# Another order of steps in each slot of a transformer encoder's software pipeline, on one core

## What is computed

```python
L, D, H, F = (4, 128, 16, 512)
for i in range(L):
    xn = layer_norm(x, ln1_w[i], ln1_b[i])
    x = x + mha(xn, mask, in_proj_w[i], in_proj_b[i], out_proj_w[i], out_proj_b[i])   # causal, ALiBi
    xn = layer_norm(x, ln2_w[i], ln2_b[i])
    h = jax.nn.gelu(xn @ ffn1_w[i].T + ffn1_b[i], approximate=False)
    x = x + (h @ ffn2_w[i].T + ffn2_b[i])
return layer_norm(x, final_w, final_b)
...
x = x + _L0_attn_ref(xn, ...) + _L0_ffn_ref(xn, ...)
```

## Time and profile before

| | us |
|---|---|
| median of three executions | 1640.66 |
| lowest, highest | 1640.59, 1646.0 |
| the profiled execution, its time | 1640.9 |
| its span in the trace | 1639.1 |
| busy in the span: PE, DVE, ACT, POOL | 1421.8, 1131.8, 1223.2, 614.3 |

### The profile page before, as it was taken

How to read it: one execution, slowest core, us unless ns; L and a number is a source line. 1 busy time by engine, 2 the same in 40 slices (tenths; PEclk the granted TensorE clock), 3 DMA queues, 4 the chain that set the end, 5 groups by cost and what they waited for, 6 DMA issues and landing times.

```text
span 1639.1 us, 38563 instructions
## 1 busy us (share of the span) xinstructions
PE 1421.8 (87%) x10720; PEld 946.2 (58%) x10720; DVE 1131.8 (69%) x2851; ACT 1223.2 (75%) x2165; POOL 614.3 (37%) x1052
## 2 busy tenths in 40 slices
PE   0677787568999999999999999999999989999995
PEld 0445554335666666666666666666666656666653
DVE  6567676347777777677677766777776767777762
ACT  3233333238999898898999888999888988888884
POOL 5232222123333343333333333334333345555443
PEclk9999888779999999999999999999999999999997
DMA  3332333045444444444444445444444444444430
GB/s 107 100 114 89 107 92 101 24 122 149 121 124 127 117 116 126 134 129 119 120 129 119 122 121 133 129 119 121 127 119 123 129 128 125 124 125 125 123 90 10
DMA packets 104789, 187.60 MB, mean 114 GB/s; under 512 B 19912, under 2 KB 70728, under 8 KB 104720
## 3 DMA queue, kind: packets, MB, share of 16 engines
q1 hardware_dynamic: 89904, 150.45, 33.3%
q0 software_dynamic: 14848, 36.72, 8.3%
HBM read 120.87 MB, written 65.01 MB: 113 GB/s over the span
## 4 chain that ended last, share of the span: by engine, by line
PE 53%; DVE 17%; issue 14%; DMA 9%; POOL 2%; DVEq 1%; ACT 1%; SPq 1%; POOLq 0%; ACTq 0%
PE pvp L979 11%; PE exp_ps L956 7%; DVE negm L698 6%; PE mxp L923 6%; PE dense L1009 6%; PE dense L1018 5%; PE dense L868 5%; DMA blocks<-split_L 4%; PE mxp L927 4%; DVE xn L666 3%; PE dense L896 2%; PE dense L997 2%; DVE ost L744 2%; PE mxp L868 2%; DMA blocks<-negt 2%
## 5 line engine op out<-in xcount | busy, mean ns | idle before, releaser
L831 ACT ACTIVATE probs<-exp_ps 128x512 f32<-128x512 f32 x896 | 525.0, 593 | 289.1 <-PE exp_ps L956 286.4
L698 DVE TENSOR_REDUCE negm<-mxp 128x2 f32<-128x512 f32 x896 | 569.2, 683 | 90.3 <-PE mxp L927 72.6
L956 PE MATMUL exp_ps<-qbd_l,kst_l 128*128 128x512 f32 x768 | 368.5, 495 | 8.3 <-issue 4.3
L923 PE MATMUL mxp<-blocks,qst 104*128 104x512 f32 x768 | 325.5, 453 | 34.5 <-DMA blocks<-split_L 19.7
L855 ACT ACTIVATE exp_ps<-masktf 128x512 f32<-128x512 f32 x513 | 308.8, 602 | 22.6 <-DVE rest L766 6.5
L927 PE MATMUL mxp<-maskb,identb 128*128 128x256 bf16 (+1 forms) x768 | 247.6, 322 | 0.0
L498 POOL TENSOR_SCALAR veps<-mv 128x2 f32<-128x2 f32 x144 | 31.7, 220 | 560.9 <-DVE mv L657 557.2
L923 PEld LDWEIGHTS mxp<-blocks,qst 104*128 104x128 f32 x768 | 149.0, 194 | 84.2 <-DVE negm L698 37.0
L979 PE MATMUL pvp<-probs,vst_l 128*32 128x256 f32 (+1 forms) x4096 | 194.5, 330 | 0.6 <-ACT probs L831 0.6
L744 DVE COPY ost<-pvp 128x512 f32<-128x512 f32 x80 | 55.3, 692 | 201.6 <-PE pvp L979 201.6
L956 PEld LDWEIGHTS exp_ps<-qbd_l,kst_l 128*128 128x128 f32 x768 | 144.4, 195 | 40.8 <-issue 31.3
(11 more groups left out here) (95 smaller groups left out, 2006.6 us busy)
## 6 DMA issues: line engine op xcount, KB each, us to landing
split_L<-hi SPq DMA_DIRECT2D x256, 128.0 KB, 2.1
qst<-split_L SPq DMA_DIRECT2D x64, 384.0 KB
kst_l<-split_L SPq DMA_DIRECT2D x64, 384.0 KB
qbd_l<-split_L SPq DMA_DIRECT2D x256, 96.0 KB
split_L<-lo POOLq DMA_DIRECT2D x128, 128.0 KB, 2.1
blocks<-split_L SPq DMA_DIRECT2D x128, 96.0 KB
blocks<-split_L POOLq DMA_DIRECT2D x128, 96.0 KB, 4.4
split_F<-hi SPq DMA_DIRECT2D x64, 128.0 KB, 2.1
```

Of the source, the lines that this page charges most:

```text
L698: dve.tensor_reduce(heads[:, g, first:first + count], mxp[:, (plan.max_chunks * g + ch) % 3, :].rearrange("p (h t) -> p h t", h=count), AX ...
L831: act.activation(probs[:, g[0], ch, :], exp_ps[:, (plan.exp_chunks * g[0] + ch) % 2, :], ACT.Exp, scale=plan.scale).then_inc(q.b_exp, 1)
L923: pe.matmul(mxp[:, bank, :], qst[0:BIAS_END, g[0], qt * P:(qt + 1) * P], kbd[0:BIAS_END, first:first + count, g[0], 0:keys], start=True, s ...
L956: pe.matmul(exp_ps[:, bank, :], kst[plan.name][:, s, g[0], kt * P:(kt + 1) * P], rhs, start=not on_diagonal, stop=True, skip_group_check=T ...
```

## The change

The steps are split into finer ones, and each has its own place in the list: `ln` and `rstd` (now at slot `s+3`), `xb`, `xb2`, `rstd2`, `y`, `hi`, `lo`, `hi>`, `row>`, `smax>`, `smaxp`, `f1` and `f2` in two halves, `gelu` in two. Since an engine takes from the list only the steps in which it has a part, each has an order of its own. A step such as `xt+` can stand in the list ahead of `xt`: ACT's part has its place among ACT's steps.

In the encoder's slot the maxima begin behind `op` and the first `pv`, and go one by one up to the slot's end. `negt` stands behind the last of them, three of the four `pv` and `v` behind it. `ln` is taken one slot earlier. `end` and `end+` stand ahead of `op+`.

Dense products use all five banks by a table `banks`; `take` makes PE wait for the bank's last reader, whoever that was. The maxima use banks 2 to 4. `SEEDER` names ACT for all eight seeds, as before. The weights come in five parts (`qk`, `v`, `o`, `w1`, `w2`), each loaded at `w:part` after its last use (`last_use`) and waited for at `w=part`; only the slots with `s == 0` wait for them. PE, ACT and DVE run the encoder in two loops, and one round earlier than before (-2).

```diff
-    def __init__(self, name, heads, causal, feed_forward, rounds):
+    def __init__(self, name, heads, causal, feed_forward, rounds, banks):
...
             return (
-                exps[0:2] + at("ot", s - 1) + at("ln", s + 2) + at("ot+", s - 1) + at("v v+", s + 1) + at("xn", s + 2)
-                + at("f2 f2+", s - 2) + at("at at+", s - 1)
-                + exps[2:3] + maxes[0:2] + at("xt", s + 2)
...
-                + exps[9:10] + at("xt2 xt2+", s - 1) + values[0:2] + end2
-                + exps[10:11] + at("negt negt+", s + 1) + at("stack_max+", s + 2)
-                + exps[11:12] + at("f1 f1+", s - 1) + values[2:4] + at("pv+", s) + store)
+                part("exp", s, 0) + at("xn", s + 2) + part("f2", s - 2, 0)
+                + part("exp", s, 1) + at("v+", s + 1) + at("w:v", s + 2) + at("ot+", s - 1) + at("ln", s + 3)
+                + at("f2+", s - 2) + end + at("xb ot", s - 1)
+                + part("exp", s, 2) + part("f2", s - 2, 1) + at("w:w2 xb2 rstd2 at at+", s - 1)
+                + end2 + at("op+ w=w1", s - 1)
+                + part("exp", s, 3, 4) + at("lo xt+", s + 2) + at("op", s - 1) + at("w:o", s) + at("stack>", s + 1)
+                + at("w=v hi>", s + 2) + part("pv", s, 0) + at("row>", s + 1) + part("max", s + 1, 0) + at("xt", s + 2)
+                + part("max", s + 1, 1)
+                + part("exp", s, 5) + at("w=w2", s - 1) + part("max", s + 1, 2) + at("rstd", s + 3)
+                + part("exp", s, 6) + at("y", s + 2) + at("xn2", s - 1) + at("qk", s + 2) + at("w:qk", s + 3)
+                + part("max", s + 1, 3) + at("hi", s + 2)
+                + part("exp", s, 7, 8) + at("w=o", s) + part("max", s + 1, 4) + at("xt2", s - 1) + at("smaxp", s + 2)
+                + part("max", s + 1, 5, 6) + at("xt2+", s - 1) + part("max", s + 1, 7)
+                + part("exp", s, 9) + part("max", s + 1, 8)
+                + part("exp", s, 10) + part("max", s + 1, 9) + part("f1", s - 1, 0) + part("max", s + 1, 10)
+                + part("exp", s, 11) + at("w=qk", s + 3) + part("max", s + 1, 11) + at("negt+", s + 1)
+                + part("gelu", s - 1, 0) + part("f1", s - 1, 1) + at("negt", s + 1) + part("pv", s, 1, 2, 3)
+                + at("smax>", s + 2) + at("pv+", s) + part("gelu", s - 1, 1) + at("w:w1", s) + at("v", s + 2) + store)
...
+    "xt": 0, "qk": 1, "v": 1, "at": 3, "op": 3, "xt2": 0, "negt": 2, "f2": 4, "ot": 0, "f1": (0, 1)})
...
+        bank = dense + [mxp[:, k, :] for k in range(3)]
...
+            def row_of_maxima(plan, q, u, s):
+                sp.wait_ge(q.b_negt, u + 1)
+                settle(sp, passed_sp)
+                wait_past(sp, q.b_s, plan.exp_chunks * GROUPS * (u - 1))
+                settle(sp, passed_sp)
+                sp.dma_start(qbd[plan.name][MAX_ROW:MAX_ROW + 1, s, :, :].bitcast(F32),
+                             negt[0:plan.heads, s, :, :].bitcast(F32)).then_inc(q.nmax[s], 16)
...
-                def dense_job(bank, sem, count, unit_offset, done=None):
-                    if read[bank] is not None:
-                        before, per_round, constant = read[bank]
+                def take(number, sem, count, unit_offset, done=None):
+                    if read[number] is not None:
+                        before, per_round, constant = read[number]
                         pe.wait_ge(before, per_round * n + constant)
-                    read[bank] = (sem, 2 * count, count * unit_offset + (count if done is None else done))
+                    read[number] = (sem, 2 * count, count * unit_offset + (count if done is None else done))
+                    return bank[number]
```

More of the change, by code:

```diff
@@ L65, in __init__ @@
         self.units = 2 * rounds
-        self.at_bank = 0 if causal else 1
     def max_bank(self, ch):
@@ L79, in at, with part @@
             return [(name, unit) for name in names.split()]
-        exps = [("exp", s, *divmod(k, self.exp_chunks)) for k in range(self.exp_chunks * GROUPS)]
-        maxes = [("max", s + 1, *divmod(k, self.max_chunks)) for k in range(self.max_chunks * GROUPS)]
-        values = [("pv", s, g) for g in range(GROUPS)]
+        def part(name, unit, *numbers):
+            return [(name, unit, k) for k in numbers]
         if self.causal:
@@ L396, in expert_round, with load_weights @@
                     share(EXPERT, S["F"], step, u, s, r)
+            q, per = S["L"], BATCH // 2
+            def load_weights(part, layer):
+                which, first, end = WEIGHTS[part]
+                to, source = (wa["L"], wa_l) if which == "a" else (wc["L"], wc_l)
+                sp.dma_start(to[:, first:end], source[layer][:, first:end]).then_inc(q.w[part], 16)
             rounds_of(sp, EXPERT, expert_round)
-            q, per = S["L"], BATCH // 2
-            sp.dma_start(wa["L"][:], wa_l[0]).then_inc(q.wa, 16)
+            for part in WEIGHTS:
+                load_weights(part, 0)
             sp.wait_ge(S["F"].c_done, BATCH)
@@ new lines, in _ @@
+            for k in (-2, -1, 0, 1):
+                encoder_round(0, k)
+            with sp.Fori(2, per - 2) as k:
+                encoder_round(0, k, inner=True)
+            encoder_round(0, per - 2)
+            encoder_round(0, per - 1)
+            with sp.Fori(1, LAYERS - 1) as layer:
+                encoder_round(layer, 0)
+                encoder_round(layer, 1)
+                with sp.Fori(2, per - 2) as k:
+                    encoder_round(layer, k, inner=True)
+                encoder_round(layer, per - 2)
+                encoder_round(layer, per - 1)
@@ L465, in _ @@
+            encoder_round(LAYERS - 1, 0)
+            encoder_round(LAYERS - 1, 1, last_layer=True)
+            with sp.Fori(2, per - 2) as k:
+                encoder_round(LAYERS - 1, k, last_layer=True, inner=True)
+            for k in range(per - 2, per + 1):
+                encoder_round(LAYERS - 1, k, last_layer=True)
             for s in range(2):
@@ L714, in steps @@
                 q = S[plan.name]
-                for step, u, s, r, g, _ in plan.steps(n, last_layer):
+                for step, u, s, r, k, _ in plan.steps(n, last_layer):
                     bt = u % BATCH if plan.causal else u
@@ L811, in steps @@
                 q = S[plan.name]
-                for step, u, s, r, g, _ in plan.steps(n):
+                chunks = plan.exp_chunks * GROUPS
+                for step, u, s, r, k, _ in plan.steps(n):
                     if step == "xt+":
@@ L838, in steps @@
                         wait_past(act, q.c_op, u - 1)
-                        act.activation(attnt[:, s, :], dense[plan.at_bank][:, 0:T], ACT.Copy).then_inc(q.c_attnt, 1)
+                        act.activation(attnt[:, s, :], bank[plan.banks["at"]][:, 0:T], ACT.Copy).then_inc(q.c_attnt, 1)
                     elif step == "xt2+":
@@ L859, in _ @@
             act.wait_ge(S["F"].c_done, BATCH)
-            seed(0)
-            rounds_of(act, ENCODER, lambda n: steps(ENCODER, n))
+            for k in range(2):
+                if SEEDER.get(k) == "ACT":
+                    seed(k)
+            encoder_rounds(act, lambda n, last_layer=False: steps(ENCODER, n))
         @block.tensor
```

443 lines of the change are left out of this document (227 added, 216 removed).

## The result

| | before | after |
|---|---|---|
| median of four executions each, us | 1643.19 | 1702.34 |
| lowest, highest | 1640.59, 1646.0 | 1700.35, 1712.29 |
| ratio of the times, 95% interval | 1 | 1.037 (1.033 to 1.042) |
| span of the profiled execution | 1639.1 | 1699.8 |

The change makes the kernel 3.7% slower. 1619 was forecast, with 1590 to 1660 as the range, and a faster kernel at 0.60: the sign was wrong, and the time lies above the range. It is near the 1698 of rival (c), the row of maxima that lands late, which had a chance of 0.14. That the two numbers meet is luck: (c)'s mechanism turns out to be about half of the loss, and two other terms make up the rest.

The account below looks back on a forecast made before the run. No engine was taken as always busy: the loop between TensorE and VectorE set the slot. Layers 0 to 2 gain 45 us; last layer loses 19, end 3, rest 1: 1640.9 to 1619, forecast 1604 to 1632, range 1590 to 1660.

Parts of the forecast that it names:

- a faster kernel: Sign of the whole: faster by more than about 8 us (under 1632.5), from forecast and rival (a); chance 0.60.
- rival (c): Slot boundary: the row lands late behind POOL's blocks, 1.3 us in all 61 slots, 1698 (1658 if half); chance 0.14.
- The row's landing: Slot boundary: 2.72 us from negt copy to the next score product, plus 0.1 for one more wait and increment.
- the sum: Whole kernel: 1640.9 - 45 (layers 0 to 2) + 19 (last layer) + 3 (end) + 1 = 1619 us.
- The walk of one slot: Undisturbed slot followed through all engines: copy at 15.5, next slot at 18.3, with 0.2 allowance 18.5 us, bounds 18.2 and 19.0.
- rival (a): Slots of layers 0 to 2: the ScalarE is the limit, not the row; slot 17.9, whole 1590; chance 0.15.
- The 1.4 us a slot: Kernel before: TensorE loses about 1.4 us per slot in short waits during the 6 us its chain runs through the VectorE.
- The last layer: Last layer's slots: op+ waits for xb behind the final norm on POOL; 21.8 us against 20.35, 19 us lost.
- Weights in five parts: Layer changes: of the 12 us estimated there, 9 go; between 0 and 12.
- The epilogue: Kernel's end: op+ of the last unit waits behind the final norm with no maxima to cover it; 3 us lost.
- The start: Start: one round more, together with the row's extra 0.1 in 16 experts' slots; 1 us lost.
- xn2: VectorE, layers 0 to 2: xn2 no longer meets POOL's lo, so about 0.6 us instead of 1.20.

Follow-up runs that it names:

- e1: Kernel after, with POOL starting its two loads of the next unit's blocks only when the row of maxima has landed; 1660.9 us, ratio 1.011.
- e10: Kernel after, with POOL's two loads issued by SP directly ahead of the row, after the copy into negt; 1750.3 us, ratio 1.063.
- e7: e6 with the first group of the values' products also moved behind the maxima, to the slot's end; 1598.6 us, ratio 0.967.
- e12: Kernel after, with xb ahead of end on POOL and end+ directly behind op+; 1668.7 us, ratio 1.014.
- e2: Kernel after, with the final normalisation late: end behind hi, end+ behind the copy into negt; 1655.5 us, ratio 1.007.
- e6: Kernel after with both repairs, e1's wait for the row and e2's late end steps; 1621.0 us, ratio 0.982.
- e3: Kernel after with the old order of steps and old banks, keeping five-part weights, finer steps and single waits; 1637.6 us, ratio 0.996.
- e8: Kernel after, with POOL's two loads of the blocks issued by SP ahead of the row on its own queue; 1673.7 us, ratio 1.014.

## Why the prediction was wrong

**The row's landing: the step that failed.** "From such a copy to the score product that waits for its row was 349.17 - 346.45 = 2.72 us in the first slot, the only place where nothing else lay between", and 0.1 was added. That row was alone on the queues, and the new order puts POOL's loads beside it; the prediction says so itself, under (c), and still built the sum on a landing of 2.2. It is 3.0, and e1 sizes it: 0.69 in 49 slots and 0.77 in 12, 43 of the 83 us between forecast and measurement. The mechanism of (c) is thus shown (POOL's loads moved behind the row, and the landing goes from 3.0 to 2.2), at somewhat more than the half of its price, for which the prediction had 1658. One reading under (c) was off: it has POOL wait only for the last maximum's product, but the timeline above has POOL wait for the landing of its own DMA of lo (1.49 us at 866.29). The chance of 0.14 was too low: all that spoke against (c) was that no row showed the two together, and its condition was read from the order itself. The Trainium skill (DMA: Bandwidth & Descriptors, Queues, rings and completion order) gave the rule by which an increment waits for every earlier write of its DMA engine, across its queues. The kernel after agrees, with its 3.0; e10 doesn't speak against it with 2.3, since there the loads' packets are through before the row's begin.

**The walk of one slot.** It has 15.5 us from score product to copy and 2.8 from there to the next, 18.3. In e1, where the row is alone, these are 15.85 and 3.08, 18.93; in the kernel after 16.21 and 3.78. So in a slot with a clean row the walk is 0.6 short (every other slot of e1 takes 19.2, and there it is 0.9). Over the 49 slots e1 has 941 us where the sum had 917: 24 us of the 58 are the walk and its allowance, and 34 the row.

The walk followed the ScalarE and the VectorE and took the ScalarE's 17.2 us as the bound. But by the same reckoning give TensorE 190.72 x 19.24 / 200 = 18.35 us, more than the ScalarE, more than the 18.2 that stood as the slot's lower end and more than the 17.9 of rival (a). In the new order TensorE's work is the chain: `op` and the first values' product, 1.5 us, stand ahead of the first maximum, which is issued at 5.8 (875.90 - 870.13); the last maximum's product at 14.5, for 14.0; and behind it half of `f1` (0.87) ahead of the transposes, which the walk let follow the last reduction at once. e7, with 0.79 us of this moved to where the row is waited for, comes to 18.53 to 18.76, the walk's 18.5; TensorE is busy for 18.33 us of the 18.53 us from 866.00 to 884.53. The 1.4 us a slot that the prediction's first paragraph has TensorE lose in the 6 us away from it don't follow from its own numbers either: 813.50 - 807.55 = 5.95, with 4.9 of work, gives 1.05. The sum doesn't use that figure.

**The last layer.** The queue on POOL was foreseen, its place and the delay: op+ comes 3.6 us later in the sum and 3.5 in the runs (8.8 us into the slot in the kernel after, 5.2 in e12). The slot came to 23.77 instead of 21.8. The row is 0.8 of the 2.0 (e1: 23.00). A term that the prediction didn't have is the next 0.9: the clock. In e1 the three slots of the last layer whose clock stays whole behind the stall take 21.92, 22.33 and 22.32 us, the other nine 23.0 to 23.5; with the same stall the fall costs 1.1 to 1.2 us, and on the mean of the twelve 0.9. e12 and e2, in which TensorE doesn't stand for 2.58 us, have 1.00.

Then 0.3 is left, and it is small because errors cancel. e6, with a clean row and late end steps, takes 20.12 us in the last layer, 0.9 more than its 19.25 before it, for which the sum had nothing; the walk adds its own shortfall; and the early end steps cost 2.0 us without the clock (23.00 - 20.12 - 0.9), where the sum had 3.3. The Trainium skill (TensorE: Matmul & The Clock Gate, HAM oscillation — how this bites in real kernels) tells of a kernel whose clock falls at each wait for data; here it is a wait for another engine, with the same 0.50, and the fall comes 9 times out of 13.

**What held.** Weights in five parts: 9 us forecast, 7 in e3 (3.6 to 9.7 by its interval). The epilogue: 3 forecast, 2.3. The start: 1, and 0.8. TensorE's wait for xn2 is gone, and POOL's xb no longer waits for the sync engine; its waits (the answer to the earlier trace rows) are for the VectorE alone:

```profile
L627 POOL TENSOR_TENSOR xb<-state,wc_l 128x128 f32<-128x128 f32 x128 | 55.8, 457 | 370.6 <-DVE state L802 370.6
```

xn2 was forecast at 0.6 for 1.20 in the earlier trace rows, since it doesn't meet POOL's lo any more; timeline of the VectorE, the same tiles now:

```profile
858.67 0.59 DVE L708 TENSOR_SCALAR xn<-state,mv,rstd 128x128 f32 x2
```

e6 comes to 1621.0, and 1619 was forecast for a kernel without the late row. That is no confirmation: its slots are 19.25 and 20.12 for 18.7 and 21.8 in the sum, so two errors cancel in it.

## What to carry to other kernels

When a new order brings a small DMA that everyone waits for next to large loads, price it with the landing under load, and look for which queue can go behind it: two lines of waiting (e1) were worth 41 us. Sum each engine's own work over the period before you follow a walk through the others; the largest of these sums, here TensorE's 18.35, is an estimate of the floor under the walk (no steady slot of these runs went below 18.5), and what counts is how much of that work stands where the row is waited for. And look behind a stall of TensorE for its second price, the granted clock of the microseconds after it: here 1.1 to 1.2 us for 2.4 to 2.6 us of standing, in most slots but not in all.

## What the runs showed of the hardware

- A 16 KB row from SP lands 3.0 us after its issue (median) with two loads of 96 KB issued by POOL 0.64 and 0.1 us ahead of it, 2.55 to 2.9 with these 1.0 to 1.2 and 0.4 to 0.6 us ahead (ten slots of e2), and 2.2 with them behind it (e1). With the same loads on SP's own queue it lands after 2.2 us (1.1 and 0.8 us ahead, e8) and 2.3 (0.9 and 0.55 us ahead, e10).
- A load's packets begin to move 1.3 us after an issue by POOL (kernel after) and 0.9 us after one by SP (e10).
- Issuing those two loads puts SP's next DMA off by 0.95 us (e10 against e1): SP's own issue time was worth more than the transfer.
- After TensorE had stood for 2.58 us in a stretch in which it was busy 3.22 of 6 us, its granted clock was 0.50 for the next 6 us, and four products took 1.71 us for 0.88. In e1 the same stall and the same 3.22 us were once followed by a clock of 1.00. Of 13 stalls of 1.8 to 2.6 us, 9 were followed by a fall in the kernel after and 10 in e1.
